# A fused conv/attention/ODE/expert block: two chunk groups instead of three in the ODE stage, and a new order of its matmuls

## What is computed

```python
def _mlp(y, W1, b1, W2, b2, W3, b3):
    h = jnp.tanh(y @ W1.T + b1)
    h = jnp.tanh(h @ W2.T + b2)
    return h @ W3.T + b3
def _rk4_step(y, dt, params):
    k1 = f(y); k2 = f(y + dt/2*k1); k3 = f(y + dt/2*k2); k4 = f(y + dt*k3)
    return y + dt * (k1 + 2*k2 + 2*k3 + k4) / 6
# y0 = x[:, 0]; 511 steps, one after the other, dt = 1/511
```

## Time and profile before

| | |
|---|---|
| median of 3 runs | 7657.05 us (7656.08 to 7659.73) |
| profiled execution | 7654.61 us, span 7652.8 us |
| mean granted TensorE clock | 0.567 |
| PE busy | 6975.1 us (91%), 201629 matmuls |
| PEld busy | 6431.8 us (84%), 144393 loads |
| DVE, ACT, POOL busy | 55%, 50%, 16% |

### The profile page before, as it was taken

One profiled execution on the slowest core, in us unless ns is written; L12 is line 12 of the kernel. 1 busy time (PEld: TensorE's weight loads), 2 busy tenths in 40 slices (PEclk: granted clock), 3 DMA queues, 4 the chain that ended last, 5 costly groups with the idle time before them and its releaser, 6 DMA issues. The chain is left out here.

```text
span 7652.8 us, 407459 instructions
## 1 busy us (share of the span) xinstructions
PE 6975.1 (91%) x201629; PEld 6431.8 (84%) x144393; DVE 4228.9 (55%) x21034; ACT 3810.8 (50%) x26434; POOL 1229.8 (16%) x5230
## 2 busy tenths in 40 slices
PE   8884999999999999999999999999999998638886
PEld 3221999999999999999999999999999997427774
DVE  5444555555555555555555555555555554448997
ACT  3331555445544554455445554455445543328886
POOL 1000222112211221222112221122112221010001
PEclk7785555555555555555555555555555555658897
DMA  1000000100010001000100001000100000012332
GB/s 49 1 20 30 4 4 4 43 5 4 4 43 5 4 4 43 5 4 4 43 5 4 4 4 43 5 4 4 43 5 4 4 23 5 0 53 111 121 123 81
DMA packets 45001, 186.93 MB, mean 24 GB/s; under 512 B 7155, under 2 KB 27318, under 8 KB 33030
## 3 DMA queue, kind: packets, MB, share of 16 engines
q1 hardware_dynamic: 38662, 145.18, 4.9%
q0 software_dynamic: 4480, 15.38, 0.6%
HBM read 122.93 MB, written 37.62 MB: 21 GB/s over the span
## 5 line engine op out<-in xcount | busy, mean ns | idle before, releaser
L851 PE MATMUL p<-H,W 128*128 128x4 f16 x130816 | 5594.8, 168 | 36.7 <-ACT h L938 20.3
L851 PEld LDWEIGHTS p<-H,W 128*128 128x128 f16 x130816 | 5577.0, 105 | 51.0 <-ACT h L938 17.3
L830 PE MATMUL p<-L,W 128*128 128x4 f16 x57232 | 5157.8, 164 | 17.7 <-issue 17.7
L1012 DVE TENSOR_TENSOR_SCAN L<-H,h 128x8 f16<-128x8 f16 x12264 | 2210.6, 181 | 2615.3 <-ACT h L938 1561.9
L938 ACT ACTIVATE H<-p 128x4 f16<-128x4 f32 x6132 | 1093.9, 179 | 1416.3 <-PE p L830 1193.9
L945 ACT ACTIVATE H<-p 128x4 f16<-128x4 f32 x6132 | 1087.6, 178 | 1401.4 <-DVE p L1024 892.9
L851 PE MATMUL p<-L,W 128*128 128x4 f16 x8176 | 1369.3, 167 | 14.5 <-issue 12.0
L938 ACT ACTIVATE h<-p 128x4 f32<-128x4 f32 x6132 | 1046.0, 171 | 4.8
L945 ACT ACTIVATE h<-p 128x4 f32<-128x4 f32 x6132 | 1044.7, 171 | 0.0
L851 PEld LDWEIGHTS p<-L,W 128*128 128x128 f16 x8176 | 850.4, 104 | 37.4 <-issue 30.8
L804 POOL TENSOR_TENSOR twice<-r 128x16 f32<-128x16 f32 x511 | 109.2, 214 | 2425.9 <-DVE r L1021 2425.9
(11 more groups left out here) (379 smaller groups left out, 4609.3 us busy)
## 6 DMA issues: line engine op xcount, KB each, us to landing
e_W<-w_scaled SPq DMA_DIRECT2D x23, 2304.0 KB
e_W<-w_scaled SPq DMA_DIRECT2D x23, 1152.0 KB, 5.2
raw_f<-in_spline SPq DMA_DIRECT2D x21, 1024.0 KB, 6.8
w_scaled<-raw_f SPq DMA_DIRECT2D x7, 2304.0 KB, 9.0
w_scaled<-raw_f SPq DMA_DIRECT2D x7, 1152.0 KB, 11.2
raw<-in_spline POOLq DMA_DIRECT2D x3, 1024.0 KB, 7.1
rows_in<-zeros POOLq DMA_DIRECT2D x4, 768.0 KB, 12.0
e_xs<-rows_in SPq DMA_DIRECT2D x12, 256.0 KB, 5.8
```

Source lines behind the costliest of these rows:

```text
L830: return pe.add_instruction(mybir.InstMatmult(name=nc.get_next_instruction_name(), engine=pe.engine, ins=[pe.lower_ap(x), pe.lower_ap(weig ...
L851: ins = pe.matmul(out[:, m, 0:B], weights, x[:, columns, 0], start=False, stop=(left[m] == 0 and part != "hl"), skip_group_check=True)
L1012: sg.up(dve.tensor_tensor_scan(flat(cols(L, GROUPS[n])), flat(cols(H, GROUPS[n])), flat(cols(h, GROUPS[n])), -1.0, ALU.mult, ALU.add), f"l ...
```

## The change

The groups become (0, 1) and (2, 3), for all engines at once, and the list of blocks is replaced. No other line is altered. The sizes of the tanhs and of the scans follow from the groups.

```diff
-    GROUPS = [(0,), (1, 2), (3,)]
+    GROUPS = [(0, 1), (2, 3)]
     G = len(GROUPS)
-    BLOCKS = [("w", 0, 2), ("h", 0, 3), ("w", 0, 0), ("w", 0, 1), ("w", 0, 3), ("h", 0, 2), ("l", 0, 2), ("hl", 0, 1),
-              ("w", 1, 0), ("w", 2, 0), ("w", 2, 3), ("hl", 0, 0), ("w", 3, 0), ("w", 3, 1), ("w", 2, 1), ("hl", 2, 0),
-              ("hl", 1, 1), ("hl", 1, 0), ("hl", 3, 0), ("w", 1, 1), ("hl", 2, 1), ("hl", 2, 2), ("hl", 3, 1), ("hl", 3, 2),
-              ("w", 3, 2), ("w", 2, 2), ("hl", 1, 2), ("l", 0, 3), ("w", 1, 2), ("w", 1, 3), ("hl", 3, 3), ("hl", 1, 3),
-              ("w", 3, 3), ("hl", 2, 3)]
+    BLOCKS = [("w", 0, 2), ("w", 1, 1), ("w", 0, 0), ("h", 0, 1), ("w", 0, 1), ("w", 1, 0), ("w", 1, 2), ("w", 0, 3),
+              ("w", 1, 3), ("h", 0, 0), ("l", 0, 1), ("hl", 1, 0), ("hl", 0, 3), ("hl", 1, 1), ("h", 3, 1), ("h", 2, 0),
+              ("w", 3, 1), ("l", 0, 0), ("h", 3, 0), ("w", 3, 0), ("w", 2, 1), ("h", 2, 1), ("w", 2, 0), ("l", 3, 0),
+              ("l", 2, 0), ("l", 2, 1), ("l", 3, 1), ("w", 2, 3), ("w", 2, 2), ("hl", 2, 2), ("w", 3, 2), ("hl", 1, 2),
+              ("hl", 2, 3), ("hl", 3, 3), ("w", 3, 3), ("hl", 1, 3), ("hl", 3, 2), ("hl", 0, 2)]
```

## The result

The changed kernel takes 7489.11 us (median of 4 runs, 7484.73 to 7496.01); beside it the kernel before took 7656.57. The ratio is 0.9781, 95% interval [0.9764, 0.9798]: 167 us saved, where 217 were forecast; 7489 lies 49 us above the forecast, 1 us inside the upper end of its own range of 7400 to 7490. It also lies in the 7480 to 7560 of rival D, so the time alone does not tell the two apart. The profiled execution took 7484.73 us.

A forecast was written before the change was run, and what follows sets the result against it. Late hand-overs (matmul, tanh, tanh, scan) stop PE in the ODE stage. Holes of 0.053, 0.006 and 0.026 go, 0.030 comes: 0.053 us a product, 217 us over 4088, giving 7440 us, range 7400 to 7490.

The forecast's parts named there:

- rival D: A second place in the product is late, such as L of the first group at position 10: 7480 to 7560 us; chance 0.09.
- Floor and holes: PE in the ODE stage: 48 matmuls at 0.0267 us, floor 1.28 a product; holes of 0.053 and 0.026 before the change.
- the rule for lateness: At PE's waits: lateness is ready time minus (start in unstopped flow minus 0.024 us).
- First wait for H of the last group: Moves from position 14 to 17; its input is 0.02 us early, so the first hole, 0.053, goes.
- First wait for L of the last group: Moves from position 23 to 26; lateness 0.030 us, so the second hole stays and alone sets the period.
- First group: Output finished at position 29; H early by 0.04 us, L at position 10 of the next product by 0.02; costs nothing.
- Turns and hiccups: PE's issue waits and first tanhs of turns in the ODE stage: zero change taken, range 0 to 5 us.
- Four more loads at nothing: Four more weight loads a product on PE, hidden under the matmul before: zero taken, 0.107 us if not hidden.
- rival A: The four added loads are not hidden and cost a slot each, 0.107 us a product: 7878 us; chance 0.03.
- Rival B: PE's clock grant in the ODE stage rises from 0.50 to 1.0: near 6320 us; chance 0.01.

The follow-up runs named there:

- groups_only: The two groups of the kernel after with the list of blocks of the kernel before: 8384.58 us, ratio 1.0954.
- shift2: Kernel after with the h's of blocks (0, 2) and (1, 2) taken from late pairs and moved forward, ACT's waits unchanged: 7603.61 us, ratio 0.9928.
- after_swap: Kernel after, with ACT waiting for PE first and DVE's seed second before the first tanh of a product: 7426.23 us, ratio 0.9702.
- after_noshare: Kernel after with its 10 pairs that share a weight load split in place, 48 loads instead of 38: 7702.88 us, ratio 1.006.
- before_swap: Kernel before, with ACT waiting for PE first and DVE's seed second before the first tanh of a product: 7650.21 us, ratio 0.9992.
- before_noshare: Kernel before with its 14 pairs that share a weight load split in place, 48 loads instead of 34: 7664.07 us, ratio 1.0012.

## Why the prediction came out, and where it did not

- *Floor and holes.* The floor of 1.281 a product, the rule for lateness and the two holes of before were right. With them groups_only came within 26 us of 8410, shift2 within 14 of 7590, after_swap's product within 0.001.
- *First wait for H of the last group.* Right: no stop at position 17.
- *First wait for L of the last group.* Its size was right (0.03, seen in after_swap), but in the kernel after it does not show: each product starts late by the first group's hole, and that uses up the lateness at 26. The forecast had said this of a miss at 10, up to 0.030.
- *First group.* This is the step that failed, although the number came near. "Tanh starts at 1.033 in layer 1" took the 0.202 from matmul to tanh from the last group; for the first it is 0.263. For layer 2 it read 0.54 by way of the scan and the seed, where in the kernel after the tanh starts 0.146 after the seed's end and waits for PE like the other. The chain to L at position 10 is 0.06 longer than counted, against 0.02 of room, so the period is set there: 1.320 instead of 1.314. The prediction held that this "costs nothing unless the chain is over 0.04 longer than its rows" (its own 0.02 and 0.030 add up to 0.05), and it was 0.06. By its own signs rival D came true, a hole at position 10 with L 0.05 or more late, to which it had given 0.09. But D reckoned with the hole at 26 on top; without it the first group costs 0.006 x 4088 = 25 us more, not 40 to 120.
- *What was luck.* That the period moved by only 0.006 is none: the last group's chain, rightly worked out, stands right behind, as after_swap shows. But the first group's miss (25 us) and that of the next point (26 us) point the same way, and that 7489 stayed below 7490 is luck; the kernel's executions run from 7485 to 7496.
- *Turns and hiccups.* "0 to 5 us" was too small. The time on top rose from 74.8 to 100.4 us, by 26: 9 from the store of expert weights in steps 54 to 59 and some 16 outside them and the turns. Of the latter the third wait of evaluation 0 is the likely main part: one of its two products takes 1.337 instead of 1.320, 511 x 0.017 = 9 us, and in after_swap, where that wait no longer comes last, the time outside the two places is 3.8 us in place of 23.4 (some 7 of this difference only because many of its products lie below its median). No run tries that wait alone.
- The two misses, 25 and 26 us, make up the 51 us between the 217 forecast and the 166 that the stage gave.
- *Four more loads at nothing.* Right as to slots: in every kernel the median distance in runs of unshared loads, away from the waits, is 0.025 to 0.028. Not right as to supply: four more loads still cost little, but with ten further ones (after_noshare) the kernel takes 214 us more. What sharing buys here is fewer instructions for PE to start: the slot is the same with and without it. That is how rival A's sign can come true by another mechanism.
- *Clock.* 0.50 in the stage, as before, whether a steady product takes 1.287 or 1.550. Rival B falls; what the Trainium skill's page "TensorE: Matmul & The Clock Gate" (Part 1) states, which the prediction set beside it, is not borne out in this stage.

## What to carry to other kernels

In a loop whose engines hand work round in a circle, work out for each wait when the result is ready and when it is asked for, with the latency read at that very hand-over. A latency borrowed from a neighbour may hide an extra wait; where an instruction has two, put the one that comes last in time on the instruction itself, that is first in the source here. Shortening one chain pays only up to the next one's slack, so an order of work and its waits have to be tuned together: the same list gave 7604 us with one order of waits and 7370 with the other.

## What was not expected of the hardware

- An instruction with a second wait starts 0.06 us later after the event than one with a single wait, if the event that comes last is the one on the separate semaphore instruction: 0.263 against 0.201 us from matmul to tanh (kernel after, first and last group). The same edit of the order made the tanh 0.06 earlier where PE's event comes last and 0.02 later where the seed does (before_swap).
- A shared weight load saves no time in a stream of 128x128 by 128x4 matmuls: 0.0267 us a matmul with and without a load.
- Somewhere above 68 loads and matmuls per us PE stalls in earnest: 24 and 26 ns a product at 68, 51 at 72, 75 at 73. Over nine tenths of these stalls lie at places 256 loads and matmuls apart, which points to the supply of instructions; that they are for fetching was not tried separately.
- Transfers that run beside PE's stream hold it up: without those of the expert weights the time on top in steps 54 to 59 falls from 38.9 to 1.2 us. This was tried in the kernels before and after alone. Of the time on top in before_noshare and after_noshare, 109 of 208 and 197 of 307 us lie outside these steps and the turns, and no run says whether they hang on transfers.
